# Orders alone in a fused SSM block: h rounded behind tanh, dt begun ahead of the output product, O in one piece, k_hi ahead of the rounded state, x1 ahead of x2

## The reference

```
mod = (silu(c) @ wmod): sa, ca, ga, sb, cb, gb for each sequence
h  = layernorm(x) * (1 + ca) + sa
u, gate = split(h @ W_in.T)
b  = u @ W_state.T;  dt = min(softplus(u @ W_dt.T + b_dt), 10)
decay = exp(-dt * rate)
state_t = decay_t * state_(t-1) + (1 - decay_t) * b_t        (scan over 512 tokens, 128 states)
z  = (state @ W_C.T) * silu(gate) + h * D
x1 = x + ga * (z @ W_out.T)
h2 = layernorm(x1) * (1 + cb) + sb;  h2_prev = h2 shifted by one token
xk, xr = mu * h2 + (1 - mu) * h2_prev, with mu_k and mu_r
k  = relu(xk @ W_k.T)^2;  r = sigmoid(xr @ W_r.T)
x2 = x1 + gb * r * (k @ W_v.T)
```

## Time and profile before

| | |
|---|---|
| median of 3 runs | 364.83 us (364.75 to 367.57) |
| the profiled execution's own time | 364.98 us |
| its span, first to last instruction | 363.1 us |
| TensorE busy | 97% of the span, 1576 matmuls |
| VectorE, ScalarE, GpSimd busy | 88%, 81%, 75% |
| TensorE's granted clock | full speed (1.0) in all 40 slices |

### The profile page before, as it was taken

One profiled execution on the slowest core, in us unless ns is written; L12 is line 12 of the kernel. 1 busy time (PEld: TensorE's weight loads), 2 busy tenths in 40 slices (PEclk: granted clock), 3 DMA queues, 4 the chain that ended last, 5 costly groups with the idle time before them and its releaser, 6 DMA issues.

```text
span 363.1 us, 5298 instructions
## 1 busy us (share of the span) xinstructions
PE 350.8 (97%) x1576; PEld 260.0 (72%) x1576; DVE 319.0 (88%) x575; ACT 294.7 (81%) x396; POOL 273.8 (75%) x257
## 2 busy tenths in 40 slices
PE   8999898999999999999999999999999999999995
PEld 4667575776868777686868768687777768688754
DVE  3878899999998999989899999989999998968846
ACT  4677678889798888979898897979889797978484
POOL 2242659969797996979799797979879697776642
PEclk9999999999999999999999999999999999999999
DMA  8942330422424042241405124140403211010013
GB/s 285 405 174 58 116 116 2 143 89 61 173 58 175 3 149 84 68 166 58 173 8 179 49 84 149 58 176 17 158 0 108 68 58 60 1 60 1 0 59 117
DMA packets 18557, 36.01 MB, mean 99 GB/s; under 512 B 4960, under 2 KB 5728, under 8 KB 18400
## 3 DMA queue, kind: packets, MB, share of 16 engines
q1 hardware_dynamic: 17808, 35.19, 28.1%
q10 hardware_dynamic: 720, 0.48, 0.4%
HBM read 27.22 MB, written 8.44 MB: 98 GB/s over the span
## 4 chain that ended last, share of the span: by engine, by line
PE 43%; ACT 26%; DVE 20%; issue 7%; POOL 2%; DMA 1%; ACTq 0%; SPq 0%; DVEq 0%; POOLq 0%
PE slot L286 38%; ACT prev L660 10%; DVE stats L886 5%; DVE state L1002 4%; ACT k_hi L818 3%; ACT k_act L831 3%; ACT silu L714 3%; DVE slot L994 3%; DVE dt L989 2%; ACT dt L683 2%; ACT z_hi L772 2%; PE slot L300 1%; DMA w_in<-weights_in 1%; ACT r_gate L649 1%; PE slot L293 1%
## 5 line engine op out<-in xcount | busy, mean ns | idle before, releaser
L1172 POOL TENSOR_TENSOR xr_lo<-xr,xr_hi 128x512 fp32r<-128x512 f32 x32 | 54.0, 1690 | 0.2 <-ACT xr_hi L704 0.2
L660 ACT ACTIVATE prev<-slot,mod,mix_prev 128x512 f32<-128x512 f32 x64 | 46.3, 786 | 0.7 <-PE slot L601 0.3
L1172 POOL TENSOR_TENSOR xk_lo<-xk,xk_hi 128x512 fp32r<-128x512 f32 x30 | 38.3, 1295 | 8.3 <-ACT xk_hi L698 8.3
L286 PE MATMUL slot<-h_hi,wf_hi 128*128 128x512 f32 x120 | 43.8, 406 | 0.0
L1207 POOL TENSOR_TENSOR rstd<-mv,half_neg 128x4 f32<-128x4 f32 x16 | 16.1, 1006 | 36.7 <-DVE mv L901 36.7
L1172 POOL TENSOR_TENSOR k_lo<-k_act,k_hi 128x512 fp32r<-128x512 f32 x30 | 38.2, 1293 | 7.3 <-ACT k_act L867 4.2
L286 PE MATMUL slot<-h_hi,wf_lo 128*128 128x512 f32 x120 | 42.6, 395 | 0.0
L1226 POOL TENSOR_TENSOR h_lo<-h,h_hi 128x512 fp32r<-128x512 f32 x28 | 35.7, 1297 | 2.4 <-ACT h_hi L679 2.4
L286 PE MATMUL slot<-h_lo,wf_hi 128*128 128x512 f32 x120 | 35.0, 396 | 0.0
L1278 POOL TENSOR_TENSOR z_lo<-z,z_hi 128x512 fp32r<-128x512 f32 x26 | 33.6, 1296 | 0.8 <-ACT z_hi L772 0.6
L951 DVE TENSOR_SCALAR xn<-slot,mv,rstd 128x256 f32<-128x256 f32 x62 | 29.2, 532 | 0.0
(11 more groups left out here) (166 smaller groups left out, 1010.3 us busy)
## 6 DMA issues: line engine op xcount, KB each, us to landing
x_ch<-x_ch_in SPq DMA_DIRECT2D x16, 512.0 KB, 3.9
x_tok<-x_tok_in SPq DMA_DIRECT2D x15, 512.0 KB, 5.4
x_out<-wmod SPq DMA_DIRECT2D x15, 512.0 KB, 3.1
spread_rows<-rows_spread SPq DMA_DIRECT2D x13, 512.0 KB, 4.1
wmod<-wmod_in SPq DMA_DIRECT2D x1, 1024.0 KB, 8.8
w_in<-weights_in SPq DMA_DIRECT2D x1, 1024.0 KB, 11.5
w_in<-weights_in SPq DMA_DIRECT2D x1, 512.0 KB, 4.7
wmod<-wmod_in SPq DMA_DIRECT2D x1, 512.0 KB, 5.7
```

The costliest lines, as they stand in the source:

```text
L286: ins = nc.tensor.matmul(out, w[:, c, at + d * P:at + (d + 1) * P], x[:, c, :], start=first, stop=last)
L660: return nc.scalar.activation(prev[:, mix, i, 1:T + 1], ps_n[:, i, :], ACT.Identity, bias=mod_at(SHIFT2 + i, k), scale=mix_prev[:, mix, i, ...
L1172: nc.gpsimd.tensor_tensor(lo, x, hi.bitcast(F32), ALU.subtract).then_inc(done, 1)
```

## The change

Only orders and the waits that belong to them; each engine issues the same instructions as before.

- TensorE: O of a sequence is done in one piece at the end of its step, low part included. The high part of `dt` of the next sequence is issued in the same step, ahead of O; its low part and all of `b`'s high part follow behind the first matmuls of the next step's k. k's low part is in one piece ahead of `b`'s low part.
- ScalarE: both halves of `z_hi` are rounded together, between the two pairs of `prev`. `h` is rounded behind tanh, ahead of the first `prev`. `k_hi` is squared ahead of the rounded state, and `k_act` directly behind it, ahead of `silu`. `offsets` stand behind the first `xk_hi`, both `xr_hi` ahead of the table load.
- VectorE: `ln1_rows` between the two mixings; x1 (`after_attention`) ahead of x2 (`residual`); `clipped` ahead of `scaled`.
- GpSimd: `ln1_rows` ahead of `second_scale`; `low_h` at the end of the step, its first half ahead of `z_lo`, its second behind.

```diff
@@ TensorE
                     half(k_out, wl_hi, MIX_K, xk_hi, 0, first=True)
                     half(k_out, wl_lo, MIX_K, xk_hi, 0)
-                if split(c):
-                    pe.wait_ge(zlo_ok[0], c - WHOLE + 1)
-                    half(o_out, wl_hi, OUT, z_lo, 0)
+                if live(b) and b > WHOLE:
+                    pe.wait_ge(hlo_ok[0], b)
+                    pe.wait_ge(hlo_ok[1], b)
+                    half(dt_out, wf_hi, 0, h_lo, 0)
+                    half(dt_out, wf_hi, 0, h_lo, 1, last=True).then_inc(dt_ps, 1)
+                    for i in range(CH):
+                        half(b_out, wf_hi, NS, h_hi, i, first=(i == 0))
+                        half(b_out, wf_lo, NS, h_hi, i)
...
-                if split(c):
-                    pe.wait_ge(zlo_ok[1], c - WHOLE + 1)
-                    half(o_out, wl_hi, OUT, z_lo, 1, last=True).then_inc(o_ps, 1)
+                if live(d) and d < LAST:
+                    for i in range(CH):
+                        pe.wait_ge(xklo_ok[i], d + 1)
+                        last = half(k_out, wl_hi, MIX_K, xk_lo, i, last=(i == CH - 1))
+                    last.then_inc(k_ps, 1)
                 if live(b) and b > WHOLE:
-                    pe.wait_ge(z_ok[0], b)
-                    pe.wait_ge(z_ok[1], b)
-                    pe.wait_ge(hhi_ok, b)
-                    for i in range(CH):
-                        half(dt_out, wf_hi, 0, h_hi, i, first=(i == 0))
-                        half(dt_out, wf_lo, 0, h_hi, i)
...
+                    half(b_out, wf_hi, NS, h_lo, 0)
+                    half(b_out, wf_hi, NS, h_lo, 1, last=True).then_inc(b_ps, 1)
...
                     half(v_out(d), wl_hi, MIX_V, k_lo, 0)
+                if live(a) and a > WHOLE:
+                    pe.wait_ge(hhi_ok, a)
+                    pe.wait_ge(z_ok[0], a)
+                    pe.wait_ge(z_ok[1], a)
+                    for i in range(CH):
+                        half(dt_out, wf_hi, 0, h_hi, i, first=(i == 0))
+                        half(dt_out, wf_lo, 0, h_hi, i)
...
                     half(o_out, wl_hi, OUT, z_hi, 1)
                     half(o_out, wl_lo, OUT, z_hi, 1)
+                    for i in range(CH):
+                        pe.wait_ge(zlo_ok[i], b - WHOLE + 1)
+                        last = half(o_out, wl_hi, OUT, z_lo, i, last=(i == CH - 1))
+                    last.then_inc(o_ps, 1)
@@ ScalarE
-                if split(c):
-                    act.wait_ge(z_ok[1], c + 1)
-                    nc.scalar.copy(z_hi[:, 1], z[:, 1]).then_inc(zhi_ok[1], 1)
                 if 0 < d < LAST:
                     rounded_xk(d, 0)
+                if live(a) and a > WHOLE + 1:
+                    offsets(a)
                 if 0 < d < LAST:
                     rounded_xk(d, 1)
-                if live(b) and b > WHOLE:
-                    rounded_h(b)
                 if live(d) and d > 0:
                     rounded_xr(d, 0)
+                    rounded_xr(d, 1)
...
-                if split_state(b) and b > WHOLE:
-                    rounded_state(b)
...
+                if split_state(b) and b > WHOLE:
+                    rounded_state(b)
+                if live(d) and c < LAST:
+                    nc.scalar.activation(k_act[:], k_act[:], ACT.Square).then_inc(kact_ok, 1)
                 if live(b):
                     if b > WHOLE:
                         gate_silu(b)
-                if live(d) and c < LAST:
-                    nc.scalar.activation(k_act[:], k_act[:], ACT.Square).then_inc(kact_ok, 1)
...
+                if live(a) and a > WHOLE:
+                    rounded_h(a)
...
                 if split(b):
-                    act.wait_ge(z_ok[0], b + 1)
                     before(act, o_ps, b)
-                    nc.scalar.copy(z_hi[:, 0], z[:, 0]).then_inc(zhi_ok[0], 1)
+                    for i in range(CH):
+                        act.wait_ge(z_ok[i], b + 1)
+                        nc.scalar.copy(z_hi[:, i], z[:, i]).then_inc(zhi_ok[i], 1)
@@ VectorE
                     mixing(c, 0)
+                if live(a + 2):
+                    ln1_rows(a + 2)
+                if live(c) and c < LAST:
                     mixing(c, 1)
...
-                if live(a + 2):
-                    ln1_rows(a + 2)
...
+                if live(b) and b < LAST:
+                    after_attention(b)
                 if live(d) and d < LAST - 1:
...
                         residual(d, i)
-                if live(b) and b < LAST:
-                    after_attention(b)
+                if live(a):
+                    clipped(a)
                 if live(a + 1):
                     scaled(a + 1)
-                if live(a):
-                    clipped(a)
@@ GpSimd
-                if live(b) and b > WHOLE:
-                    low_h(b)
...
+                if live(a + 1):
+                    ln1_rows(a + 1)
                 if c == LAST:
...
                     low_state(b)
-                if live(a + 1):
-                    ln1_rows(a + 1)
...
+                if live(a) and a > WHOLE:
+                    low_h(a, 0)
                 if split(b):
...
+                if live(a) and a > WHOLE:
+                    low_h(a, 1)
```

More of the change, by code:

```diff
@@ L478, in _ @@
                     half(k_out, wl_lo, MIX_K, xk_hi, 1)
-                if split(c):
-                    pe.wait_ge(zlo_ok[1], c - WHOLE + 1)
-                    half(o_out, wl_hi, OUT, z_lo, 1, last=True).then_inc(o_ps, 1)
-                if live(b) and b > WHOLE:
-                    pe.wait_ge(z_ok[0], b)
-                    pe.wait_ge(z_ok[1], b)
-                    pe.wait_ge(hhi_ok, b)
-                    for i in range(CH):
-                        half(dt_out, wf_hi, 0, h_hi, i, first=(i == 0))
-                        half(dt_out, wf_lo, 0, h_hi, i)
-                if live(d) and d < LAST:
-                    pe.wait_ge(xklo_ok[0], d + 1)
-                    half(k_out, wl_hi, MIX_K, xk_lo, 0)
-                if live(b) and b > WHOLE:
[L493 to L498, removed]
-                if live(b) and b > WHOLE:
[L500 to L503, removed]
+                if live(d) and d < LAST:
[3 more added lines that the diff above has]
+                    last.then_inc(k_ps, 1)
+                if live(b) and b > WHOLE:
+                    half(b_out, wf_hi, NS, h_lo, 0)
+                    half(b_out, wf_hi, NS, h_lo, 1, last=True).then_inc(b_ps, 1)
                 if 1 < c < LAST:
@@ L513, in _ @@
                     half(r_out, wl_lo, MIX_R, xr_hi, 0)
-                if live(b) and b > WHOLE:
-                    half(b_out, wf_hi, NS, h_lo, 0)
-                    half(b_out, wf_hi, NS, h_lo, 1, last=True).then_inc(b_ps, 1)
                 if live(b) and b > WHOLE:
@@ L769, in _ @@
                 a, b, c, d = s, s - 1, s - 2, s - 3
-                if split(c):
-                    act.wait_ge(z_ok[1], c + 1)
-                    nc.scalar.copy(z_hi[:, 1], z[:, 1]).then_inc(zhi_ok[1], 1)
                 if 0 < d < LAST:
                     rounded_xk(d, 0)
+                if live(a) and a > WHOLE + 1:
+                    offsets(a)
                 if 0 < d < LAST:
                     rounded_xk(d, 1)
-                if live(b) and b > WHOLE:
-                    rounded_h(b)
                 if live(d) and d > 0:
                     rounded_xr(d, 0)
+                    rounded_xr(d, 1)
                 if live(b) and b > WHOLE:
                     nc.scalar.preload_act_table_set("natural_log_exp_and_others")
[L783 to L789, removed]
+                    exponential(b)
                 if live(d) and d < LAST:
@@ L1220, in low_state, with low_h @@
                 nc.gpsimd.tensor_tensor(state_lo[:], state[:], state_hi[:].bitcast(F32), ALU.subtract).then_inc(slo_ok, 1)
[L1222 to L1225, removed]
-                    nc.gpsimd.tensor_tensor(h_lo[:, i], h[:, k % 2, i], h_hi[:, i].bitcast(F32), ALU.subtract).then_inc(hlo_ok[i], 1)
+            def low_h(k, i):
+                pool.wait_ge(hhi_ok, k)
+                pool.wait_ge(g_ps, k)
+                nc.gpsimd.tensor_tensor(h_lo[:, i], h[:, k % 2, i], h_hi[:, i].bitcast(F32), ALU.subtract).then_inc(hlo_ok[i], 1)
             ln1_scale(0)
@@ L1236, in _ @@
             ln1_rows(WHOLE + 1)
-            low_h(2)
+            low_h(2, 0)
+            low_h(2, 1)
             second_scale(0)
```

## The result

The changed kernel takes **367.68 us** (median of 19 runs, 366.79 to 369.87), the kernel before 365.36 (19 runs, 364.75 to 367.57): ratio **1.0063**, interval 1.0048 to 1.0077. So it is 0.6% slower, by more than its uncertainty and by less than 1%. The forecast was 368. The span of the profiled execution is 364.9 us against 363.1, 1.8 longer.

A forecast was written before the change was run, and what follows sets the result against it. Bound: a 21.03 us ring through TensorE, VectorE and ScalarE; opening it gains 0.8 per step, the held second h costs 1.0. 364.98 + 12 x 0.24 + 1.0 - 0.15 = 368 us, own range 365 to 371, overall 354.5 to 371.5.

The forecast's parts named there:

- The old ring: Chain through TensorE, VectorE and ScalarE's row work up to the second z_hi, 21.03 us a step; opening it gains 0.8.
- The second `h`: On VectorE, k_lo gets in between the two h and holds the second: +1.0 us per step.
- Rival B: No collision between k_lo and the h pair: ring 20.27 us, total 356 us (352 to 359); chance 0.25.
- C: k_lo meets only the tail of h or waits: 0.3 to 0.7 of the 1.0 paid, 359 to 365; chance 0.08.
- The ring's size: New ring through TensorE and VectorE: 21.27 us per step with the collision, 20.27 without, against 21.03 before.
- this sign, 21.1 to 21.4: Sign that the forecast is right: exponentials of successive steps 21.1 to 21.4 us apart.
- The edges: Opening step +1.9 and +0.7 us, closing step -1.6; taken as +1.0, bounds -1 and +2.
- parts 3 and 4: Earlier h rounding and h_lo; x1 ahead of x2, clip ahead of scaled, ln1_rows moved: each part worth nothing.
- TensorE's idle time ahead of `dt`: Sign that the forecast is right: about 1.1 us idle per step before dt's first matmul, released by VectorE's z.
- ScalarE's wait for the scan gone: Sign that the forecast is right: k_hi fills ScalarE's idle 1.47 us before the rounded state, so this wait disappears.
- The signs of being wrong in kind: Decay, not statistics, last at the drive; or TensorE waiting for h_lo, z_lo or xk_hi over 0.3 us per step.
- D: GpSimd work also collides with VectorE's mean-and-variance instructions, 0.3 to 0.8 us per step: 372 to 378 us; chance 0.12.

The follow-up runs named there:

- experiment 1: Changed kernel with one added wait: GpSimd begins k_lo only when both h of the step are done; 356.24 us, ratio 0.975.
- experiment 2: Changed kernel with ScalarE squaring k_act behind silu again, no wait added; 355.15 us, ratio 0.9738.
- experiment 4: Kernel before with k_hi ahead of the rounded state, k_act directly behind it, and GpSimd's ln1_rows ahead of second_scale; 374.93 us, ratio 1.0277.
- experiment 9: Kernel before with k_hi ahead of the rounded state and GpSimd's ln1_rows early, k_act left behind silu; 362.62 us, ratio 0.9922.
- Experiment 10: Changed kernel with GpSimd's ln1_rows behind the second xr_lo in the opening step alone; 366.32 us, ratio 1.0022.
- experiment 7: On top of experiment 2, x2 ahead of x1 again on VectorE; 355.4 us, ratio 0.9734.
- experiment 3: Changed kernel with GpSimd's ln1_rows back between low_state (state_lo) and k_lo; 368.49 us, ratio 1.009.

## Why the prediction was right

The forecast's case was the one that came, and its mechanism is shown: the second `h`, held by `k_lo`, eats what the opened ring gives. But much of the closeness of the two numbers, 368 and 367.68, is luck. The sum as written, 364.98 + 12 x 0.24 + 1.0 - 0.15, is 368.7, which I put down as 368. It makes the change +3.9 us, where the medians give +2.3 and the spans +1.8, and the kernel before stood 0.5 us higher in its further runs. By its steps:

- **The old ring opens, a new one takes its place.** Shown by the chain. `z_hi` doesn't release TensorE in the steady steps any more (7.1 us in 13 waits before, one wait of 0.7 after), and ScalarE has idle time in front of the relu (17.5 us in 14 times, before 3.6 in one).
- **The second `h`.** Said: 1.7 to 1.9 us with `k_lo` directly behind `state_lo`; measured: 1.78, the pair 2.49 against 2.45. Experiments 1, 2, 4 and 9 show from both kernels that this collision alone makes 11 to 12.5 us. The undisturbed pair is a little longer than the "about 1.35" of the prediction: 1.42 in the opening of the changed kernel; no term rests on it. Rival B is what experiment 1 measured, 356.24; its sum is 356.7, put down as 356. C, a part of the price, did not come: all twelve pairs pay it whole.
- **The ring's size.** Said 21.27, measured 21.06; without the collision said 20.27, measured 20.08 and 20.00, where TensorE's own work is the bound. By terms: statistics to `xn` 4.17, measured 4.02; `xn` and `h` 4.24, measured 4.29; TensorE with the gating and z 12.86, measured 12.75. The first is the one most mis-sized, and the reason is that I read it off a single step. That step was the odd one: in the kernel before, the other steady steps take 4.01 to 4.02 from the statistics to `xn`. The changed kernel has one such step too, at the same place, the one after the step shown here. It takes 4.20, with a gap of 0.21 us within the mean-and-variance instructions, whose cause stays open. VectorE's timeline:

```profile
202.72 0.17 DVE L887 SCALAR_TENSOR_TENSOR mv<-mv,stats 128x4 f32<-128x4 f32 x1 [0.21 <-DVE mv L885]
```

  Of +0.24 per step 0.03 was left by the k matmuls (said +2.9 us in twelve steps, measured +0.4), and nothing by the exponentials, which are 21.02 apart in the mean. So this sign, 21.1 to 21.4, was missed.
- **The edges.** Said +1.0, measured +3.38 - 1.96 = +1.42. The closing was 0.36 better than said (-1.6) and the opening 0.8 worse than its +2.6. Experiment 10 gives `xr_lo` 1 behind the row work 1.1 to 1.4 us, where I had 0.7: half of that 0.8 or more.
- **"Nothing" for parts 3 and 4.** Right for x1 and x2 (experiment 7). Of the row work it was right only as a pair with `offsets`: without the collision the kernel is at 368.49 with late row work (experiment 3) and at 355.15 or 356.24 with early (experiments 2 and 1).
- **TensorE's idle time ahead of `dt`.** Said 1.1 us, measured 0.99, released by z.
- **ScalarE's wait for the scan gone.** Wrong: it is 10.9 us in 14 times, where it was 17.1. `k_hi` fills part of it, and it sits off the ring now.
- **The signs of being wrong in kind.** Neither came. The statistics are the last to arrive at the drive: in the step shown the decay is done at 180.64 and the drive begins at 181.83, directly behind them. TensorE has no steady wait for `h_lo`, `z_lo` or `xk_hi`.
- **D, a second collision.** It did not come: none of the mean-and-variance instructions of the twelve steady steps exceeds 0.17. But the room was small. GpSimd's row work took 2.7 us, not 1.5, and ended at 201.26, 1.0 us ahead of the first of them (202.27).

The Trainium skill says in GPSIMD Engine Reference, section 8 Key points, that GpSimd shares its SBUF interfaces with VectorE, with contention where a VectorE instruction reads two SBUF inputs, as `h` does, or runs in a 2-port mode. The runs agree. That page has no price for it; here it is one `h` of 1.78 us instead of 0.74.

## What to carry to other kernels

Before moving an instruction earlier, ask which third engine it releases: `k_act` stood on the chain that ended last neither in the changed kernel nor in experiment 2, 4 or 9, and still its place alone was worth 12 us, since it set whether GpSimd met VectorE's two `h` from the front or from the back. Where such a meeting can't be avoided, let the engine that has slack come second; even a semaphore wait added for that gave 3.1% here (356.24 against 367.68). And a row of a typical step should be compared with a few others before it is multiplied by twelve.

## What the runs showed of the hardware

- **Where `k_lo` and `h` meet, the handover lies at instruction borders.** A `k_lo` that was issued during the first of two queued `h` runs ahead of the second (after, experiment 4); one issued during the second waits for its end (experiments 2 and 9). The one that comes second waits for the other's end, and shows that wait as its own time: `h` 1.78 us instead of 0.74, `k_lo` 1.80 instead of 1.30.
- **It takes other VectorE instructions along, but not those that read PSUM.** The clip, 128x512 on SBUF, has a median of 0.56 us in the changed kernel, 0.72 in the one before and 1.13 in experiment 2 (417 to 1455 ns over the three): the instruction is the same, and what GpSimd does beside it differs. That it is the same cause is argued from the lines, not tried. The four `xn` of a step, which read PSUM, take 519 to 541 ns each in the whole run of the changed kernel, with `state_lo` beside them too, and the gating, which reads SBUF and PSUM, 1.21 to 1.23 us in all twelve traces, in the changed kernel with the second `k_lo` beside it.
- **A second `h` that is held still has work left after the grant.** From the end of the first `h` (185.50 + 0.87 = 186.37) to that of the second (188.07) are 1.70 us. The first `k_lo` ends at 187.51, 1.14 us behind the first `h`, and the second `h` 0.56 us later. From the opening I had worked out 1.13 and 0.55.
